# A row bias moved from TensorE into the residual buffer, with the residual added by an accumulating DMA

## The chip, the cores and the metric

The kernel runs on 8 cores of one Trainium2 chip. Core c computes half h = c mod 2 of sequence c // 2, so every core does the same work on 2048 rows of its own (and a few rows around them). The cores don't talk to each other. The metric is the device time of the slowest core, in microseconds.

## What is computed

One layer on x of shape (4, 4096, 1024), float32: windowed attention with 16 query heads and 2 key heads, a layer norm of the sum with x, a gated feed-forward block that mixes each row with the row before it, and a second layer norm.

```python
q, k, v = x @ Wq + bq, x @ Wk + bk, x @ Wv + bv        # 16, 2 and 2 heads of 64
scores = einsum('bgrsd,bgswd->bgrsw', qg, k_win)       # a window of 256 keys about each row
out = softmax(scores) @ v_win
x1 = layernorm(x + out @ Wo + bo)
x_prev = shift(x1, 1)
r = sigmoid((mu_r * x1 + (1 - mu_r) * x_prev) @ W_r.T)
k = (mu_k * x1 + (1 - mu_k) * x_prev) @ W_k.T
y = layernorm(x1 + r * (square(relu(k)) @ W_v.T))
```

The change is about `bo`, the bias of the output projection, and about how the `x +` of the third last group of lines is brought in.

## The kernel before, in words

The work of a core is written out as 172 slots (`NSLOT`). A planner (`plan_units`, `plan_rows`) fixes ahead of time which unit of work falls in which slot, and each engine's program is a loop over the same slots. Up to slot 131, each slot holds one step of attention: TensorE makes the scores of 64 rows of two pairs of heads (`qk`, L231, L237), VectorE takes the row maxima (`max_step`, L529), ScalarE the exponentials (`exp_step`, L383), VectorE scales them (`normalise`, L534, L541). Every fourth slot TensorE multiplies by the values (`av`, L344) and ScalarE evicts the result into `ao` (`ao_out`, L441). Beside these steps the slots hold units of projections: K and V (L270), q (L276), the feed-forward products k, r, v (L301, L309, L319), and the output projection o. Their results go through three PSUM banks in turn (`pm`), evicted by ScalarE or VectorE, and a unit waits for the eviction of the unit three before it.

**The output projection.** For each of 17 blocks tau of 128 rows there are two units ("o", tau, 0) and ("o", tau, 1), one for each half of the 1024 columns. They stand in slots 15, 16 for tau = 0 and 8 tau + 10, 8 tau + 11 for the others. Each is eight products `ao` x `w16o` of 128x128 by 128x512 (L289), and a ninth product of a single row, `ones` (1x128) by `bo16` (1x512), which adds the bias (L291). VectorE then adds `zx`, which holds x, and writes the sum back into `zx` with a row total (L565). `zx` has two buffers, tau mod 2.

**The first layer norm.** ScalarE squares `zx` in slot SQ1[tau] (`squares_1`, L464), GpSimd computes mean and scale with 128x1 operations (`layer_norm`, L675 to L687), ScalarE writes the normalised rows into `qy` in slot YOUT[tau] = SQ1[tau] + 2 (`rows_y`, L469). Then `zx` is free, and x of block tau + 2 is loaded into it: GpSimd waits for `s_y` in slot YOUT[tau] + 1 and issues the DMA (L698). The first two blocks are loaded after the weights w16o (L662). YOUT is 19, 22, 30, 38, 46, 54, 62, 70, 79, 86, 94, 102, 110, 118, 126 for the fifteen blocks that a load follows.

**The second layer norm.** Its squares stand in slots SQ2 (73, 76, 87, 88, 99, 103, 112, 115, 125, 128, ...; `squares_2`, L481), GpSimd computes its scale one slot later in program order (L725 to L728, the operations at L678 to L687), and ScalarE writes the rows two slots after SQ2, in slots FIN (75, 78, 89, 90, 101, 105, 114, 117, ...; `rows_out`, L486).

**The queues.** GpSimd issues, in program order: w16k, four pieces of x for group 0, the four pieces of wq with mask and ident between them, w16v, x of group 1, w16o, the bias, the first two `zx`; then, slot by slot, first the first layer norm, then the load of `zx` (L698), then at most one piece of x or of the feed-forward weights, then the second layer norm. SyncE (SP) issues `cols`, and then slot by slot: from slot 73 on, in every odd slot, a DMA transpose of probabilities (`p_transpose`, L739), due at the `av` four or so slots later; in slots 48 + 13 h and 50 + 13 h a DMA transpose of normalised rows (`y_transpose`, L747), which needs the transpose before it into the same buffer to have landed (L746), and which VectorE needs for `shift_diff` (L591, L595) in slot 52 + 13 h; and the output DMA after each FIN (L767). All DMAs of a core share its 16 DMA engines.

Of the kernel before, what the change touches and what calls it, by code (L numbers as in the profile page):

```python
# [9 lines left out]
ALU = mybir.AluOpType  # L10

D = 1024
KC = 8
# [96 lines left out]
def build_nc():  # L110
# [19 lines left out]
    wkf_in = dram("wkf", [KC, 128, D])  # L130
    wvf_in = dram("wvf", [KC, 128, D])
    cols_in = dram("cols", [128, 32])
    bo_in = dram("bo", [1, D])
    mask_in = dram("mask", [128, 2, 64])
    ident_in = dram("ident", [128, 256])
    out = dram("out", [T, D], "ExternalOutput")
# [21 lines left out]
    junk = sb("junk", [128, D])  # L158
    mask = sb("mask_s", [128, 2, 64])
    ident = sb("ident_s", [128, 256])  # L160
    bo16 = sb("bo16", [1, D])
    ones = sb("ones", [1, 128])
    cols = sb("cols_s", [128, 32], F32)
    bkm = sb("bkm", [128, 4], F32)
    nmax = sb("nmax", [128, 4, 2], F32)
# [25 lines left out]
    mur_s, muk_s = cols[:, 12:20], cols[:, 20:28]  # L191


    d_cols, d_mask, d_ident, d_bo = sem("d_cols"), sem("d_mask"), sem("d_ident"), sem("d_bo")
    d_wk, d_wv, d_wo = sem("d_wk"), sem("d_wv"), sem("d_wo")
    d_wr, d_wkf, d_wvf = sem("d_wr"), sem("d_wkf"), sem("d_wvf")
    d_wq = [sem("d_wq%d" % j) for j in range(4)]
# [23 lines left out]
    def tensor(e):  # L221
# [19 lines left out]
        def unit(u):  # L241
# [38 lines left out]
            elif kind == "o":  # L280
                if b == 0:
                    e.wait_ge(s_ao, 2 * a + 1)
                if a == 0 and b == 0:
                    e.wait_ge(s_cst, 1)
                if a == 0 and b == 0:
                    e.wait_ge(d_wo, 128)
                    e.wait_ge(d_bo, 16)
                for kc in range(KC):
                    e.matmul(pm[:, bank, :], ao[:, a % 2, kc, :], w16o[:, kc, 512 * b:512 * b + 512],  # L289
                             start=(kc == 0), stop=False)  # L290
                mm = e.matmul(pm[:, bank, :], ones[:, :], bo16[:, 512 * b:512 * b + 512],  # L291
                              start=False, stop=True)
            elif kind == "k":
                if b == 0:
                    e.wait_ge(s_mix, 8 * a + 8)
                if a == 0 and b == 0:
                    e.wait_ge(d_wkf, 128)
                for j in range(2):
                    dc = 2 * b + j
                    for kc in range(KC):  # L300
                        mm = e.matmul(pm[:, bank, 256 * j:256 * j + 256],  # L301
                                      w16kf[:, kc, 128 * dc:128 * dc + 128],
                                      xk[a % 2][:, kc, :],
                                      start=(kc == 0), stop=(kc == KC - 1))
            elif kind == "r":
                if a == 0 and b == 0:
                    e.wait_ge(d_wr, 128)
                for kc in range(KC):
                    mm = e.matmul(pm[:, bank, :],  # L309
                                  xr[(a // 2) % 2][:, kc, 128 * (a % 2):128 * (a % 2) + 128],  # L310
                                  w16r[:, kc, 512 * b:512 * b + 512],
                                  start=(kc == 0), stop=(kc == KC - 1))
            else:
                if a % 2 == 0 and b == 0:
                    e.wait_ge(s_ka, 4 * (a // 2) + 4)
                if a == 0 and b == 0:
                    e.wait_ge(d_wvf, 128)
                for kc in range(KC):
                    mm = e.matmul(pm[:, bank, :],  # L319
                                  kact[(a // 2) % 2][:, kc, 128 * (a % 2):128 * (a % 2) + 128],  # L320
                                  w16vf[:, kc, 512 * b:512 * b + 512],
                                  start=(kc == 0), stop=(kc == KC - 1))
# [190 lines left out]
                    evac(u)  # L513

    def vector(e):
        e.memset(ones[:, :], 1.0)
        e.memset(vt[:, 0:64], 0.0)
        e.memset(vt[:, 64 + XC:128 + XC], 0.0)
        e.memset(ao[:, 0, :, 0:64], 0.0)
# [105 lines left out]
    def gpsimd(e):  # L625
# [3 lines left out]
        def wq_piece(j):  # L629
            e.dma_start(wq[j], wq_in.ap()[j]).then_inc(d_wq[j], 16)  # L630

        def wo_piece(c):
            e.dma_start(w16o[:, c, :], wo_in.ap()[c]).then_inc(d_wo, 16)

# [22 lines left out]
        e.wait_ge(d_xt[1], 64)  # L657
        for c in range(5, 8):
            wo_piece(c)
        e.dma_start(bo16[:, :], bo_in.ap()).then_inc(d_bo, 16)  # L660
        for j in range(2):
            e.dma_start(zx[:, j, :], xres.ap()[128 * j:128 * j + 128, :]).then_inc(d_xres[j], 16)  # L662

        def small(ins, s=s_p):
            nonlocal n_p
# [24 lines left out]
        for n in range(NSLOT):  # L690
            if n - 1 in SQ1:
                tau = SQ1.index(n - 1)
                e.wait_ge(s_sq1, tau + 1)
                layer_norm(st1[:, tau % 2, :], True, tau == 0, s_ln1)
            if n - 1 in YOUT[:NT - 2]:
                tau = YOUT.index(n - 1)
                e.wait_ge(s_y, tau + 1)
                e.dma_start(zx[:, tau % 2, :], xres.ap()[128 * (tau + 2):128 * (tau + 3), :]) \  # L698
                    .then_inc(d_xres[tau % 2], 16)
            piece = 3 * ((n - 12) // 4) + (n - 12) % 4 if n >= 12 and (n - 12) % 4 < 3 else -1  # L700
            if 0 <= piece < 36:
                e.wait_ge(s_ex, n)
# [26 lines left out]

    def sync(e):  # L730
        e.dma_start(cols[:, :], cols_in.ap()).then_inc(d_cols, 16)

        def p_transpose(b, pair):
            r = b % 2
# [15 lines left out]
        for n in range(NSLOT):  # L750
# [4 lines left out]
            if 0 <= h < NH and f in (0, 2):  # L755
# [3 lines left out]
                if f == 0 and h >= 1:  # L759
                    e.wait_ge(s_pc, h)  # L760
                y_transpose(2 * h + 1 + f // 2, par, 64 * f, 2 * (h // 2) + par + f // 2)
            if n - 1 in FIN:
                r = FIN.index(n - 1)
                e.wait_ge(s_o, r + 1)
# [54 lines left out]
def _host_inputs(L0_attn_x, L0_attn_Wq, L0_attn_bq, L0_attn_Wk, L0_attn_bk,  # L819
# [16 lines left out]
        wr=_by_chunks(np.asarray(L0_ffn_W_r, np.float32).T),  # L836
        wkf=_by_chunks(np.asarray(L0_ffn_W_k, np.float32).T),
        wvf=_by_chunks(np.asarray(L0_ffn_W_v, np.float32).T),
        bo=np.ascontiguousarray(np.asarray(L0_attn_bo, np.float32).reshape(1, D)),
        mask=mask,  # L840
        ident=np.concatenate([np.tile(np.eye(64, dtype=np.float32), (2, 2)),
                              np.eye(128, dtype=np.float32)], 1),
# [38 lines left out]
```

## Time and profile before

| what | value |
|---|---|
| time, median of 3 runs | 510.87 us (510.54 to 511.59) |
| the profiled execution's own time | 509.77 us |
| its span on the slowest core (core 5) | 508.2 us |
| spans of the 8 cores | 504.9 to 508.2 us |
| busy: TensorE / ScalarE / VectorE / GpSimd | 87% / 66% / 62% / 21% of the span |
| granted TensorE clock, mean | 0.960 of full speed |
| DMA: moved, mean rate | 48.25 MB, 95 GB/s |

The span is first to last instruction of one core; the device time of the same execution is 1.57 us longer. Busy shares are means over stages with different limits. In a row that merges instructions, the first number is the start and the second the time to the end of the last of them.

### The profile page before, as it was taken

Reading aid. Unit: us, or ns where it says so; the run is one execution under the profiler, and the core shown is the slowest. Engines: PE = TensorE matmul, PEld = TensorE weight load, DVE = VectorE, ACT = ScalarE, POOL = GpSimd, SP = SyncE. Lnnn points to the kernel's source line nnn. Section 1 sums busy time; section 2 is a strip of 40 time slices with the busy share of each in tenths; the row PEclk is TensorE's granted clock in tenths of the full one; section 3 lists DMA queues with packets and bytes.
Section 4 is the critical chain, followed back from the end, with each engine's and each line's share of the span. In section 5 each row is a group of like instructions: output and inputs, shape, how many; then the busy total and the mean of one; then the engine's idle time right before and its main releaser. Section 6 shows DMA issues by size and latency. Waiting matters only on the chain.

```text
span 508.2 us, 10503 instructions; the slowest of 8 cores (504.9 to 508.2 us)
## 1 busy us (share of the span) xinstructions
PE 440.9 (87%) x3052; PEld 220.6 (43%) x3052; DVE 316.5 (62%) x793; ACT 333.3 (66%) x847; POOL 109.0 (21%) x298
## 2 busy tenths in 40 slices
PE   0779999999899869798898988998979988999990
PEld 0344444444444345444363353353435345464640
DVE  0056765654655587576967877877776896545421
ACT  1267868686768575776679496669658769446542
POOL 4330124130403030101122230121123032130303
PEclk9996999999999878899999999999989999999996
DMA  8999429939263646100265286567254548303112
GB/s 108 164 164 195 62 44 115 161 64 140 28 110 54 113 73 117 40 5 1 66 139 135 52 100 156 110 84 187 53 115 115 135 53 177 90 1 103 43 42 83
DMA packets 71448, 48.25 MB, mean 95 GB/s; under 512 B 59104, under 2 KB 60256, under 8 KB 71392
## 3 DMA queue, kind: packets, MB, share of 16 engines
q0 software_dynamic: 11632, 24.88, 28.1%
q1 hardware_dynamic: 59760, 22.70, 22.7%
q8 instruction: 26, 0.43, 0.4%
q14 instruction: 30, 0.25, 0.2%
HBM read 40.85 MB, written 8.39 MB: 97 GB/s over the span
## 4 chain that ended last, share of the span: by engine, by line
PE 59%; ACT 15%; DVE 9%; issue 8%; DMA 5%; POOL 1%; ACTq 0%; SPq 0%; DVEq 0%; POOLq 0%
PE pm L289 11%; PE pm L276 8%; PE pm L319 8%; PE pm L309 6%; PE pm L301 6%; PE po L344 6%; ACT p L383 5%; PE psc L231 4%; DVE nmax L529 4%; PE pm L255 3%; DMA bufq<-wq 2%; PE pm L291 2%; ACT junk L464 2%; DMA yT<-qy 2%; PE pm L270 1%
## 5 line engine op out<-in xcount | busy, mean ns | idle before, releaser
L383 ACT ACTIVATE p<-psc,nmax 128x320 bf16<-128x320 f32 x264 | 138.8, 540 | 96.1 <-DVE nmax L529 95.9
L529 DVE TENSOR_REDUCE nmax<-psc 128x2 f32<-128x640 f32 x132 | 108.1, 821 | 88.8 <-PE psc L237 88.2
L289 PE MATMUL pm<-w16o,ao 128*128 128x512 bf16 x272 | 66.3, 388 | 2.5 <-ACT ao L441 1.2
L541 DVE TENSOR_SCALAR p<-p,rall 128x320 bf16<-128x320 bf16 x264 | 62.4, 299 | 7.6 <-DVE rall L534 0.7
L276 PE MATMUL pm<-bufx,bufq 128*128 128x512 bf16 (+2 forms) x320 | 65.1, 350 | 1.7 <-DMA bufq<-wq 1.7
L301 PE MATMUL pm<-bufx,w16kf 128*128 128x256 bf16 x512 | 62.4, 278 | 2.1 <-ACT pt L397 1.5
L309 PE MATMUL pm<-w16r,bufx 128*128 128x512 bf16 x256 | 59.6, 379 | 5.0 <-DVE zx L565 2.2
L319 PE MATMUL pm<-w16vf,bufq 128*128 128x512 bf16 x256 | 59.5, 380 | 1.8 <-ACT pt L397 1.8
L383 ACT ACTIVATION_READ_ACCUMULATOR p<-psc,nmax 128x1 f32 x264 | 57.1, 216 | 0.0
L301 PEld LDWEIGHTS pm<-bufx,w16kf 128*128 128x128 bf16 x512 | 48.7, 99 | 14.1 <-issue 8.0
L231 PE MATMUL psc<-k,qy 64*128 64x320 bf16 x264 | 41.7, 313 | 13.5 <-ACT p L383 13.1
L276 PEld LDWEIGHTS pm<-bufx,bufq 128*128 128x128 bf16 x320 | 28.6, 100 | 30.0 <-issue 9.4
L255 PE MATMUL pm<-ident_s,p 128*128 128x128 bf16 x360 | 34.2, 230 | 7.2 <-ACT qy L421 4.8
L289 PEld LDWEIGHTS pm<-w16o,ao 128*128 128x128 bf16 x272 | 24.9, 98 | 33.4 <-issue 8.5
L676 POOL TENSOR_TENSOR st<-st 128x1 f32<-128x1 f32 x17 | 3.8, 224 | 162.5 <-ACT junk L464 162.5
L571 DVE SCALAR_TENSOR_TENSOR zb<-bufq,pm 128x512 f32<-128x512 f32 x32 | 21.8, 683 | 26.6 <-PE pm L319 26.6
L309 PEld LDWEIGHTS pm<-w16r,bufx 128*128 128x128 bf16 x256 | 23.2, 97 | 33.7 <-issue 9.4
L344 PE MATMUL po<-pt,v 128*64 128x256 bf16 (+1 forms) x396 | 37.0, 292 | 0.2 <-issue 0.2
L565 DVE SCALAR_TENSOR_TENSOR zx<-pm,zx 128x512 f32<-128x512 f32 x34 | 23.4, 688 | 21.5 <-PE pm L291 21.3
L319 PEld LDWEIGHTS pm<-w16vf,bufq 128*128 128x128 bf16 x256 | 23.3, 98 | 30.6 <-issue 5.5
L255 PEld LDWEIGHTS pm<-ident_s,p 128*128 128x128 bf16 x360 | 23.9, 102 | 23.4 <-issue 20.1
L231 PEld LDWEIGHTS psc<-k,qy 64*128 64x128 bf16 x264 | 13.2, 93 | 41.7 <-issue 34.4
(80 smaller groups left out, 572.4 us busy)
## 6 DMA issues: line engine op xcount, KB each, us to landing
zx<-xres POOLq DMA_DIRECT2D x17, 512.0 KB, 6.3
out<-zb SPq DMA_DIRECT2D x16, 512.0 KB, 3.2
bufx<-xt POOLq DMA_DIRECT2D x16, 256.0 KB, 8.9
bufq<-wq POOLq DMA_DIRECT2D x4, 512.0 KB, 10.0
w16o<-wo POOLq DMA_DIRECT2D x8, 256.0 KB, 11.8
w16kf<-wkf POOLq DMA_DIRECT2D x8, 256.0 KB, 5.8
w16r<-wr POOLq DMA_DIRECT2D x8, 256.0 KB, 6.1
w16vf<-wvf POOLq DMA_DIRECT2D x8, 256.0 KB, 6.5
```

The costliest lines, as they stand in the source:

```text
L231: e.matmul(psc[:, 2 * (n % 2) + g, 0:320], qb[64 * g:64 * g + 64, b + 1, 2 * j:2 * j + 2, :], k16[64 * g:64 * g + 64, 64 * b:64 * b + 320] ...
L255: mm = e.transpose(pm16[:, bank, 128 * c:128 * c + 128], src[:, 128 * c:128 * c + 128], eye)
L276: mm = e.matmul(pm[:, bank, 0:QHI[a] - QLO[a]], wq[b // 2][:, kc, 128 * (b % 2):128 * (b % 2) + 128], xt[:, a % 2, kc, QLO[a]:QHI[a]], sta ...
L289: e.matmul(pm[:, bank, :], ao[:, a % 2, kc, :], w16o[:, kc, 512 * b:512 * b + 512], start=(kc == 0), stop=False)
L301: mm = e.matmul(pm[:, bank, 256 * j:256 * j + 256], w16kf[:, kc, 128 * dc:128 * dc + 128], xk[a % 2][:, kc, :], start=(kc == 0), stop=(kc ...
L309: mm = e.matmul(pm[:, bank, :], xr[(a // 2) % 2][:, kc, 128 * (a % 2):128 * (a % 2) + 128], w16r[:, kc, 512 * b:512 * b + 512], start=(kc ...
L319: mm = e.matmul(pm[:, bank, :], kact[(a // 2) % 2][:, kc, 128 * (a % 2):128 * (a % 2) + 128], w16vf[:, kc, 512 * b:512 * b + 512], start=( ...
L344: mm = e.matmul(po[64 * g:64 * g + 64, :].rearrange("p (s k q) -> p k s q", k=2, q=128)[:, kind, :, :], v16[lo:hi, (b + kind) % 2, vc, 64 ...
L383: a = e.activation(p16[:, b % 2, j // 2, g, j % 2, :], psc[:, 2 * (n % 2) + g, 0:320], AF.Exp, bias=nmax[:, n % 4, g:g + 1], accum_out=sal ...
L529: e.tensor_reduce(nmax[:, n % 4, :], psc[:, 2 * (n % 2):2 * (n % 2) + 2, 0:320], mybir.AxisListType.X, ALU.max, negate=True).then_inc(s_mx, 1)
L541: t = e.tensor_scalar(part, part, rall[:, b % 2, r:r + 1], None, ALU.mult)
L565: e.scalar_tensor_tensor(z, src, 1.0, z, ALU.mult, ALU.add, accum_out=st1[:, a % 2, b:b + 1]).then_inc(s_ed, 1)
```

## The change

`bo` becomes an input of 128 equal rows (`np.tile` on the host), 512 KB. The products of `ones` by `bo16` are gone, with both tiles, the memset of `ones` and the load of `bo16` (2 KB) on GpSimd. SyncE copies the 128 bias rows into `zx` (a "fill"): both buffers right at the start after `cols`, and later in slot YOUT[tau] + 1 once `rows_y` of block tau is done. GpSimd waits for the fill (`d_bo`) and then issues the load of x as a DMA that adds to what is in `zx`: for the first two where they stood, for the others one slot later than before, YOUT[tau] + 2. In a slot that holds both, it comes after the first layer norm and ahead of the second one, as before. Within SyncE's slot the fill comes after `p_transpose` and `y_transpose` and ahead of the output DMA. The bias fills read 17 x 512 KB more from memory.

```diff
-    bo_in = dram("bo", [1, D])
+    bo_in = dram("bo", [128, D])
...
-    bo16 = sb("bo16", [1, D])
-    ones = sb("ones", [1, 128])
...
-                    e.wait_ge(d_bo, 16)
                 for kc in range(KC):
-                    e.matmul(pm[:, bank, :], ao[:, a % 2, kc, :], w16o[:, kc, 512 * b:512 * b + 512],
-                             start=(kc == 0), stop=False)
-                mm = e.matmul(pm[:, bank, :], ones[:, :], bo16[:, 512 * b:512 * b + 512],
-                              start=False, stop=True)
+                    mm = e.matmul(pm[:, bank, :], ao[:, a % 2, kc, :], w16o[:, kc, 512 * b:512 * b + 512],
+                                  start=(kc == 0), stop=(kc == KC - 1))
...
     def gpsimd(e):
+        def add_xres(tau):
+            e.wait_ge(d_bo[tau % 2], 16 * (tau // 2 + 1))
+            e.dma_start(zx[:, tau % 2, :], xres.ap()[128 * tau:128 * tau + 128, :],
+                        accum_op=ALU.add).then_inc(d_xres[tau % 2], 16)
...
-        e.dma_start(bo16[:, :], bo_in.ap()).then_inc(d_bo, 16)
         for j in range(2):
-            e.dma_start(zx[:, j, :], xres.ap()[128 * j:128 * j + 128, :]).then_inc(d_xres[j], 16)
+            add_xres(j)
...
-            if n - 1 in YOUT[:NT - 2]:
-                tau = YOUT.index(n - 1)
-                e.wait_ge(s_y, tau + 1)
-                e.dma_start(zx[:, tau % 2, :], xres.ap()[128 * (tau + 2):128 * (tau + 3), :]) \
-                    .then_inc(d_xres[tau % 2], 16)
+            if n - 2 in YOUT[:NT - 2]:
+                add_xres(YOUT.index(n - 2) + 2)
...
     def sync(e):
         e.dma_start(cols[:, :], cols_in.ap()).then_inc(d_cols, 16)
+        for j in range(2):
+            e.dma_start(zx[:, j, :], bo_in.ap()).then_inc(d_bo[j], 16)
...
                 y_transpose(2 * h + 1 + f // 2, par, 64 * f, 2 * (h // 2) + par + f // 2)
+            if n - 1 in YOUT[:NT - 2]:
+                tau = YOUT.index(n - 1)
+                e.wait_ge(s_y, tau + 1)
+                e.dma_start(zx[:, tau % 2, :], bo_in.ap()).then_inc(d_bo[tau % 2], 16)
```

## Rows read from the trace of the kernel before

**Rows 1.** The page: span, TensorE's busy time, the chain that ended last
```profile
span 508.2 us, 10503 instructions; the slowest of 8 cores (504.9 to 508.2 us)
PE 440.9 (87%) x3052; PEld 220.6 (43%) x3052; DVE 316.5 (62%) x793; ACT 333.3 (66%) x847; POOL 109.0 (21%) x298
...
PE 59%; ACT 15%; DVE 9%; issue 8%; DMA 5%; POOL 1%; ACTq 0%; SPq 0%; DVEq 0%; POOLq 0%
PE pm L289 11%; PE pm L276 8%; PE pm L319 8%; PE pm L309 6%; PE pm L301 6%; PE po L344 6%; ACT p L383 5%; PE psc L231 4%; DVE nmax L529 4%; PE pm L255 3%; DMA bufq<-wq 2%; PE pm L291 2%; ACT junk L464 2%; DMA yT<-qy 2%; PE pm L270 1%
```
**Rows 2.** Line L291: count, shortest/median/longest in ns, first and last start
```profile
L291 PE MATMUL pm<-bo,ones x34: 384/385/602, 63.7 to 450.8; 1*128 1x512 bf16 x34
```
**Rows 3.** Timeline of TensorE about one bias product (start, us, engine, line)
```profile
63.69 0.39 PE L291 MATMUL pm<-bo,ones 1*128 1x512 bf16 x1
64.01 0.45 PE L255 MATMUL pm<-ident_s,p 128*128 128x128 bf16 x5
```
**Rows 4.** Timeline of the start: first DMAs, TensorE's first two waits
```profile
1.06 0.39 SPq L731 DMA_DIRECT2D cols_s<-cols  x1
1.55 0.74 POOL L635 DMA_DIRECT2D w16k<-wk  x1 [0.87 <-POOLq L111]
...
14.05 3.26 PE L270 MATMUL pm<-bufx,w16k 128*128 128x512 bf16 x8 [14.05 <-DMA bufx<-xt]
...
21.59 1.46 PE L276 MATMUL pm<-bufx,bufq 128*128 128x384 bf16 x8 [1.68 <-DMA bufq<-wq]
```
**Rows 5.** Stretches: PE, PEld, DVE, ACT, POOL busy, PEclk, DMA share, GB/s
```profile
0.00:2.00 2.00, 0.00 (x0) 0.00 (x0) 0.80 (x5) 0.94 (x1) 0.63 (x5) 1.00 0.00 0
6.00:8.00 2.00, 0.00 (x0) 0.00 (x0) 0.00 (x0) 0.00 (x0) 0.63 (x2) 1.00 1.12 161
244.00:245.00 1.00, 1.00 (x8) 0.34 (x8) 1.00 (x4) 0.00 (x0) 0.00 (x0) 1.00 0.65 115
245.00:246.00 1.00, 1.00 (x15) 0.50 (x14) 0.60 (x1) 0.00 (x0) 0.00 (x0) 1.00 0.97 397
```
**Rows 6.** The page's DMA issues: KB each, median us from issue to landing
```profile
zx<-xres POOLq DMA_DIRECT2D x17, 512.0 KB, 6.3
out<-zb SPq DMA_DIRECT2D x16, 512.0 KB, 3.2
```
**Rows 7.** Timelines of ACT, SP and POOL about slots 86 to 89
```profile
293.69 1.24 ACT L469 ACTIVATE qy<-zx,st 128x1024 bf16<-128x1024 f32 x1
...
289.48 7.14 SPq L739 DMA_TRANSPOSE pt<-p  x2
296.82 1.45 SPq L747 DMA_TRANSPOSE yT<-qy  x1
...
295.48 0.62 POOL L698 DMA_DIRECT2D zx<-xres  x1 [3.16 <-ACT qy L469]
297.15 0.18 POOL L678 TENSOR_SCALAR st<-st 128x1 f32<-128x1 f32 x1 [1.05 <-ACT junk L481]
...
299.31 0.29 POOL L687 TENSOR_TENSOR st<-st 128x1 f32<-128x1 f32 x1
...
301.64 1.27 ACT L486 ACTIVATE zb<-zb,st 128x1024 f32<-128x1024 f32 x1
```
**Rows 8.** Timelines of SP, POOL and ACT about slots 103 to 105
```profile
344.34 7.39 SPq L739 DMA_TRANSPOSE pt<-p  x2
...
349.79 0.26 POOL L687 TENSOR_TENSOR st<-st 128x1 f32<-128x1 f32 x1
...
351.70 1.34 ACT L486 ACTIVATE zb<-zb,st 128x1024 f32<-128x1024 f32 x1
```
**Rows 9.** Waits for transposes: VectorE and TensorE timelines, the chain
```profile
309.18 0.18 DVE L591 COPY yT<-yT 128x8 bf16<-128x8 bf16 x1 [3.43 <-DMA yT<-qy]
...
312.46 1.89 PE L309 MATMUL pm<-w16r,bufx 128*128 128x512 bf16 x8 [1.42 <-DVE zx L565]
...
421.20 6.25 DMA yT<-qy
```

More of the change, by code:

```diff
@@ L191, in build_nc @@
     mur_s, muk_s = cols[:, 12:20], cols[:, 20:28]
-    d_cols, d_mask, d_ident, d_bo = sem("d_cols"), sem("d_mask"), sem("d_ident"), sem("d_bo")
+    d_cols, d_mask, d_ident = sem("d_cols"), sem("d_mask"), sem("d_ident")
+    d_bo = [sem("d_bo%d" % j) for j in range(2)]
     d_wk, d_wv, d_wo = sem("d_wk"), sem("d_wv"), sem("d_wo")
@@ L515, in vector @@
     def vector(e):
-        e.memset(ones[:, :], 1.0)
         e.memset(vt[:, 0:64], 0.0)
@@ L838, in _host_inputs @@
         wvf=_by_chunks(np.asarray(L0_ffn_W_v, np.float32).T),
-        bo=np.ascontiguousarray(np.asarray(L0_attn_bo, np.float32).reshape(1, D)),
+        bo=np.ascontiguousarray(np.tile(np.asarray(L0_attn_bo, np.float32).reshape(1, D), (128, 1))),
         mask=mask,
```

## The prediction

> **What bounds the kernel now.** I read the page first, then the chain of waits, then the timelines of the places that the edits touch. TensorE is busy 440.9 of 508.2 us [rows 1], and the chain that ended last lies on it for 59% of the span, on ScalarE for 15%, on VectorE for 9%, on DMA for 5% [rows 1]. So TensorE is what mostly sets the pace, with ScalarE close behind: time taken from TensorE is worth something, and time added to ScalarE costs something. The line of the bias products, L291, has 2% of that chain [rows 1], about 10.2 us. At the start nothing computes: TensorE first waits 14.05 us for weights and x, and again for wq until 21.59 [rows 4]; the DMA engines' share in the stretch from 6 to 8 us is over 1 [rows 5]. That stage is bound by DMA, and the change puts 1 MB into it.
>
> The times below are those of the profiled execution: 508.2 us span, 509.77 us device time, 1.10 us below the median of 510.87. I sum against 509.77 and carry the difference to the median.
>
> **Taken away: 34 bias products.** Each lasts 385 ns [rows 2] and overlaps the next. What the path gives is from start to start: L291 starts at 63.69, the unit after it at 64.01 [rows 3], so 0.32 us each, 34 x 0.32 = 10.9 us in all. The chain's 10.2 us say that 32 of the 34 were on it. Not all of that comes back. Once TensorE is ahead, ScalarE (333.3 us busy, and in some slots without a gap) or the loop scores, maxima, exponentials holds it at the next wait. Upper bound 10.9 us; as lower bound I take half of the chain's share, 5 us, which would need a shadow behind every second product. TensorE's 59% against ScalarE's 15% put it nearer the upper end: **-8.0**. The wait for `bo16` and the memset go too; the weight load dominates the wait and the memset precedes the first DMA landing, so 0.
>
> **Added at the start: two fills of 512 KB.** What one costs the DMA engines I read from a load of the same size in a quiet place: one at 242.67 us (the eighth of fifteen at its line) shows as shares of 0.65 and 0.97 of two successive microseconds [rows 5], so 1.6 to 1.7 us of all 16 engines. Two make 3.4 us. SyncE is free from 1.45 us [rows 4], before GpSimd's first load can get going, and until 2 us the engines do nothing [rows 5]. About 1 us of the fills may fall into this gap; the rest pushes w16k, x and wq back, and with them all that follows. Bounds 0 (the fills fit in gaps) and +3.4; nearest is the row of the full DMA stretch, so **+2.5**. That stretch writes 161 GB/s as bf16, read as twice as many bytes of f32 [rows 5], some 320 GB/s.
>
> The Trainium skill, page "HBM Reference", section "Specifications (TRN2)", gives a core about 358 GB/s when both cores of a pair stream. By that rule 1.05 MB cost an estimated 2.9 us, not 3.4, and the sum would be half a microsecond better at most; the trace's 320 GB/s lies below that limit.
>
> **Moved: SyncE's fill, then GpSimd's wait for it.** A fill goes the way of the output DMA: same queue, size and partitions, 3.2 us from issue to landing [rows 6]. Upper bound is the 6.3 us of the loads of x [rows 6]. The GpSimd load used to need `s_y` only. Now GpSimd stands still until the fill has landed, with the second layer norm queued behind it where SQ2 follows YOUT closely. The planner's numbers give two such places, slots 88 and 104; at 112/113 and 128/129 the squares come a slot later and cover most of the wait, and early on only weight pieces stand behind it, all due many slots later.
>
> *Slot 88.* `rows_y` ends at 294.93, but in slot 87 SyncE first issues two transposes; the second of them starts at 296.82 and takes 1.45 [rows 7]. So the fill is issued at about 298.4, behind them in the same queue, and lands 3.2 to 3.6 later, at about 302. GpSimd then issues the adding load (0.62 us) and starts the layer norm at 302.8. That took from 297.15 to 299.60 [rows 7], 2.45 us, so it ends at 305.3. ScalarE wants it at 301.64 [rows 7]: a stall of 3.7 us. The next layer norm (SQ2 88) then ends at 307.8 and is wanted at 304.78 + 3.7, no second stall. Against it stands a wait that may shrink: `y_transpose`, issued at 296.82 next to the load of x, landed so late that VectorE lost 3.43 us at 309.18, and TensorE 1.42 us [rows 9]. The load of x no longer collides with it, and the path has that much slack. Taken: 3.7 - 1.4, about **+2.5** (0 if the fill slips ahead and ScalarE had other slack, +6 with a landing of 6.3).
>
> *Slot 104.* `p_transpose` starts at 344.34 [rows 8], issued for 1.35 us; the fill lands at about 349.2, the load is issued, the layer norm ends at 352.3 to 352.8. It ended at 350.05 and is wanted at 351.70 [rows 8]: 1.1 us of stall, of which part is slack: **+0.6** (0 to +3.6).
>
> **More traffic beside the transposes.** Per block the engines now carry a fill (1.7 us) and an adding load. What such a load costs no row shows. Bounds: 1.7 us, that of a plain one, and 3.4, if both streams that it reads count in full. I take 2. Loads are due at slot 8 tau + 26 and are issued ten slots before; 6.3 us plus 3 are hidden there, and for the first one (five slots, some 13 us) just so. The `d_bo` of the first two was served long before. The transposes are not so covered: the one at 421.20, on the chain, took 6.25 us [rows 9] beside a load of x. Now a fill stands right ahead of it in its queue instead, and the add comes after it. Taken: **+0.8** (-1.5 if the collision goes, +4 if three or four places lose 1 us each).
>
> The Trainium skill, page "DMA: Bandwidth & Descriptors", section "SDMA does more than copy", says that the DMA engines add in units inline with the data stream; by that rule the adding load costs what a plain one does. No run here shows it yet.
>
> **SyncE's waits.** The fills put waits for `s_y` ahead of `y_transpose` 0 to 4, which ran far ahead before. The fill of slot 47 waits to about 162 us, their consumer stands in slot 52, after 179: some 10 us of room, cost 0; without that room VectorE would wait.
>
> **Sum:** -8.0 + 2.5 + 2.5 + 0.6 + 0.8 = -1.6 us. 509.77 becomes 508.2; the median 510.87 becomes **509.3 us**.
>
> **The rivals.**
>
> *The fills are hidden.* The first DMA data would flow before w16k wants the engines, GpSimd's wait would end in time, and TensorE's gain comes whole: -10.2 + 1 + 1.5 + 0.5 = -7.2, to about 503.7; half way, 505.5. For it: TensorE's share of the chain. Against it: the full DMA stretch at the start, and the order in SyncE's slot 87.
>
> *GpSimd's hold decides (slower).* Its place is the wait for the fill ahead of the layer norm in slots 88 and 104, its price the landing time. At 6.3 us, as for the loads of x, the stalls are 6.4 - 1.4 = 5.0 and 3.6 us, the sum -8.0 + 2.5 + 5.0 + 3.6 + 0.8 = +3.9, or 514.8. It turns the sign from a landing of about 4.5 us. For it: these fills are issued right behind transposes, when the engines are busy. Against it: 3.2 us for the output DMA on the same queue. With a landing of 5.5 it is about 513.
>
> *The gain is absorbed.* TensorE's 0.32 us are lost each time to ScalarE, the gain is 5 to 6 us, the losses as above: +0.5 to +1.4, so 511.3 to 512.3. For it: ScalarE runs without a gap in the stretch about slots 88 and 104. Against: 32 of 34 products on the chain.
>
> **How the numbers follow.** Forecast case, 507.5 to 511: chance 0.45. Fills hidden, 503.5 to 507: 0.20. GpSimd's hold, 512 to 515: 0.20. Gain absorbed, 510.5 to 512.5: 0.15. About 0.2%, 1 us, is what a measurement can tell from no change here. Faster by more: 0.28 of the forecast case and the 0.20, 0.48. Within: 0.15 of the forecast case and 0.08 of the absorbed one, 0.23. Slower: 0.02 + 0.20 + 0.07, 0.29. The range 505.0 to 514.0 leaves out the far end of each side, and its halves follow the bounds: 4.3 us down are the full gain with half-hidden fills, 4.7 up a landing of near 6 us.
>
> **What would show it.** L291 is gone and 34 units are 0.32 us shorter. TensorE's first product moves from 14.05 to about 16.5. In slots 88 and 104 ScalarE's L486 waits for GpSimd's L687, by about 3.7 and 1.1 us, and GpSimd waits for a DMA into `zx`. The landing of fills (3.2 to 3.6) and of adding loads (6 to 8). A start that does not move, fills that land in over 4.5 us, or no wait at L486 would make it wrong, each with a step of its own.

## The result: slower by 2%, and the profile after

The changed kernel takes 1.0195 times the time of before, 95% interval 1.0163 to 1.0226; its median is 521.03 us. It is slower beyond doubt; whether by more than 2% the interval leaves open. Ratios and intervals compare executions in which all cores held their usual clock: in two of five of the changed kernel a die or both ran at a lower one, and these took 541 and 560 us. In the profiled execution the device time is 521.47 us, 11.7 us above the 509.77 of before. The forecast was 509.3 with a range up to 514.0, so both the sign and the size were wrong.

The page after: span, engines, the chain that ended last by engine and by line, the two DMA queues, the group of the adding loads, and three lines of DMA issues.

```profile
span 519.8 us, 10424 instructions; the slowest of 8 cores (508.3 to 519.8 us)
PE 428.0 (82%) x2976; PEld 221.8 (43%) x3018; DVE 316.7 (61%) x792; ACT 332.6 (64%) x847; POOL 113.0 (22%) x297
...
q0 software_dynamic: 11600, 24.88, 30.9%
q1 hardware_dynamic: 62208, 31.61, 27.2%
...
PE 51%; DMA 11%; DVE 11%; ACT 11%; issue 9%; POOL 3%; SPq 2%; ACTq 0%; DVEq 0%; POOLq 0%
PE pm L287 9%; PE pm L275 8%; PE pm L305 7%; PE pm L315 7%; DMA yT<-qy 5%; PE po L340 5%; PE pm L297 5%; PE psc L230 4%; DVE nmax L524 4%; ACT p L379 3%; PE pm L254 3%; DMA bufq<-wq 2%; DMA zx<-bo 2%; DMA w16k<-wk 2%; ACT junk L460 2%
...
L629 POOL DMA_DIRECT2D zx<-xres x17 | 15.4, 928 | 117.7 <-DMA zx<-bo 116.7
...
zx<-bo SPq DMA_DIRECT2D x17, 512.0 KB, 4.5
zx<-xres POOLq DMA_DIRECT2D x17, 512.0 KB, 6.5
out<-zb SPq DMA_DIRECT2D x16, 512.0 KB, 3.1
```

Three things are to be seen against [rows 1]. TensorE's busy time fell (440.9 to 428.0 us; some records of this core are missing), while the span grew by 11.6. On the chain TensorE fell from 59% to 51%, and DMA rose from 5% to 11%, GpSimd from 1% to 3%: what TensorE gave, waits took. And the spans of the cores, which lay within 3.3 us of each other, now lie within 11.5. The metric is the slowest core, so this spread is part of the loss: on the mean of the eight cores the span grew by 6.8 us and not by 11.6. A fill lands in 4.5 us at the median, not in the 3.2 of the output DMA [rows 6].

To find where the time went, I read the starts of `rows_y` and `rows_out` on ScalarE's timeline, whose slots are known, and took differences. In us, mean of the eight cores of each profiled execution ("a" is the changed kernel, e1 to e12 are the experiments below); the last row is the slowest core:

| stretch | before | e1 | a | e2 | e3 | e10 | e12 | e8 | e9 | e5 |
|---|---|---|---|---|---|---|---|---|---|---|
| to slot 19 | 76.3 | 75.9 | 77.8 | 78.5 | 78.7 | 77.9 | 78.2 | 75.0 | 74.8 | 75.6 |
| 46 to 54 | 26.1 | 25.3 | 29.9 | 24.8 | 30.5 | 31.4 | 31.5 | 33.2 | 25.6 | 24.8 |
| 86 to 89 | 7.9 | 7.9 | 13.1 | 13.5 | 7.9 | 7.9 | 9.6 | 8.0 | 7.9 | 7.9 |
| 89 to 94 | 17.1 | 17.1 | 15.9 | 16.6 | 15.6 | 14.8 | 17.9 | 17.5 | 17.3 | 16.3 |
| 102 to 105 | 8.7 | 8.7 | 11.5 | 12.2 | 8.7 | 8.7 | 10.0 | 8.7 | 8.7 | 8.7 |
| 105 to 110 | 15.4 | 14.5 | 15.5 | 15.2 | 14.5 | 14.5 | 14.2 | 14.5 | 14.6 | 14.5 |
| 127 to 130 | 8.7 | 8.7 | 11.3 | 11.5 | 8.7 | 11.6 | 8.7 | 8.7 | 8.7 | 8.7 |
| 130 to 134 | 10.5 | 10.5 | 8.2 | 8.2 | 10.7 | 7.9 | 10.5 | 10.7 | 10.5 | 10.8 |
| to slot 168 | 500.1 | 490.3 | 507.0 | 504.5 | 497.9 | 497.9 | 502.8 | 497.2 | 489.4 | 489.5 |
| slowest core | 501.6 | 494.1 | 513.3 | 508.6 | 503.4 | 502.1 | 505.3 | 505.2 | 491.1 | 495.7 |

The fair comparison is with e1, the kernel before without its bias products. Against it the changed kernel loses 4.6 us about slot 52, 5.1 before slot 89, 2.9 before slot 105 and 0.9 right behind it, 2.7 before slot 130, and 1.9 at the start. Not all of it stays: from 89 to 94 it is 1.1 us shorter than e1, and from 130 to 134 it is 2.3 shorter, so that the wait before slot 130 is made up but for 0.3 us.

The cores differ in more than one stretch. Between core 2 (508.8 us) and core 6 (519.8) 2.5 us lie in 46 to 54, 3.0 in 38 to 46 and 1.7 in 105 to 110, and the last two go with TensorE's clock. After the wait before slot 105 it fell on six cores and stayed up on cores 2 and 4. The stretch 105 to 110 on core 2 and on core 6, with columns as in [rows 5]:

```profile
354.68:368.90 14.22, 12.36 (x74) 5.14 (x75) 9.69 (x26) 10.02 (x28) 2.04 (x7) 1.00 0.49 114
```
```profile
360.91:376.82 15.91, 13.89 (x73) 5.54 (x75) 9.22 (x25) 10.01 (x29) 2.04 (x7) 0.89 0.45 104
```

**Slot 88.** The timelines of SyncE, GpSimd and ScalarE of core 6, and two stretches with their columns as in [rows 5]:

```profile
299.74 1.28 SPq L745 DMA_TRANSPOSE yT<-qy  x1
301.11 0.54 SPq L763 DMA_DIRECT2D zx<-bo  x1
...
306.04 0.90 POOL L629 DMA_DIRECT2D zx<-xres  x1 [10.82 <-DMA zx<-bo]
306.70 0.47 POOL L677 TENSOR_SCALAR st<-st 128x1 f32<-128x1 f32 x1
...
309.35 0.19 POOL L686 TENSOR_TENSOR st<-st 128x1 f32<-128x1 f32 x1 [0.43 <-POOL st L685]
...
309.63 1.24 ACT L482 ACTIVATE zb<-zb,st 128x1024 f32<-128x1024 f32 x1 [4.97 <-POOL st L686]
...
308.00:310.00 2.00, 0.00 (x0) 0.00 (x0) 0.00 (x0) 0.37 (x1) 1.26 (x5) 0.78 0.55 83
310.00:312.00 2.00, 0.50 (x2) 0.26 (x3) 0.00 (x0) 2.00 (x5) 1.15 (x5) 0.50 1.05 209
```

This is the chain that the prediction worked out for [rows 7]: transposes, then the fill at 301.11, GpSimd's issue only at 306.04, the layer norm, and ScalarE 4.97 us late. From the fill's issue to GpSimd's next step it is 4.9 us and not 3.6. TensorE then has nothing to do from 305.7 to 311.5, and when it goes on its granted clock is 0.50, the lower of its two levels (1.2 and 2.4 GHz), for some 4 us.

**Slot 52.** The timelines of SyncE and VectorE and the chain (start, us, what) of the same core:

```profile
78.77 84.40 SPq L763 DMA_DIRECT2D zx<-bo  x5
163.27 11.69 SPq L745 DMA_TRANSPOSE yT<-qy  x3
...
165.41 7.29 DMA yT<-qy
172.77 12.22 DMA yT<-qy
...
185.22 0.24 DVE L586 COPY yT<-yT 128x8 bf16<-128x8 bf16 x1 [6.74 <-DMA yT<-qy]
```

The three transposes of rows 0 to 2, which had left at 77, 87 and 111 us, now leave from 163.27, right behind the fifth fill. They have some 15 us; but one lands after 7.29 us, the next, which must wait for it, after 12.22, and VectorE stands still for 6.74 us; on the eight cores it is 4.1 to 7.7.

That such a transpose can take this long stood already in the trace before. There, on core 5, the same three leave beside weights and x and take 11.0 to 15.8 us, which nobody notices, as they are wanted only at 179 us. The line of DMA issues for the stretch 76 to 113 us of core 5 before (median to landing):

```profile
yT<-qy SPq DMA_TRANSPOSE x3, 11.4
```

### The profile page after: what moved, and what is told of

The parts are those of the page before. It is cut to its first block, busy times and chain, and to the rows that moved or that the text cites. A ratio compares the mean times of both kernels' runs of the same rounds, so it can differ in the third digit from the quotient of the medians.

```text
span 519.8 us, 10424 instructions; the slowest of 8 cores (508.3 to 519.8 us)
## 1 busy us (share of the span) xinstructions
PE 428.0 (82%) x2976; PEld 221.8 (43%) x3018; DVE 316.7 (61%) x792; ACT 332.6 (64%) x847; POOL 113.0 (22%) x297
## 4 chain that ended last, share of the span: by engine, by line
PE 51%; DMA 11%; DVE 11%; ACT 11%; issue 9%; POOL 3%; SPq 2%; ACTq 0%; DVEq 0%; POOLq 0%
PE pm L287 9%; PE pm L275 8%; PE pm L305 7%; PE pm L315 7%; DMA yT<-qy 5%; PE po L340 5%; PE pm L297 5%; PE psc L230 4%; DVE nmax L524 4%; ACT p L379 3%; PE pm L254 3%; DMA bufq<-wq 2%; DMA zx<-bo 2%; DMA w16k<-wk 2%; ACT junk L460 2%
## 5 line engine op out<-in xcount | busy, mean ns | idle before, releaser
L315 PE MATMUL pm<-w16vf,bufq 128*128 128x512 bf16 x247 | 58.1, 379 | 2.9 <-ACT pt L393 2.0
L379 ACT ACTIVATION_READ_ACCUMULATOR p<-psc,nmax 128x1 f32 x264 | 55.5, 210 | 0.0
L230 PE MATMUL psc<-k,qy 64*128 64x320 bf16 x264 | 41.7, 313 | 14.2 <-ACT p L379 13.9
L254 PE MATMUL pm<-ident_s,p 128*128 128x128 bf16 x360 | 33.5, 227 | 13.2 <-ACT qy L417 10.9
L287 PEld LDWEIGHTS pm<-w16o,ao 128*128 128x128 bf16 x272 | 25.3, 100 | 44.0 <-issue 20.0
L275 PEld LDWEIGHTS pm<-bufx,bufq 128*128 128x128 bf16 x320 | 29.3, 102 | 31.3 <-issue 11.6
L629 POOL DMA_DIRECT2D zx<-xres x17 | 15.4, 928 | 117.7 <-DMA zx<-bo 116.7
L305 PEld LDWEIGHTS pm<-w16r,bufx 128*128 128x128 bf16 x256 | 23.9, 99 | 35.1 <-issue 11.3
L340 PE MATMUL po<-pt,v 128*64 128x256 bf16 (+1 forms) x396 | 38.4, 300 | 0.1
L254 PEld LDWEIGHTS pm<-ident_s,p 128*128 128x128 bf16 x360 | 24.8, 101 | 29.8 <-issue 23.2
L560 DVE SCALAR_TENSOR_TENSOR zx<-pm,zx 128x512 f32<-128x512 f32 x34 | 23.4, 687 | 15.8 <-PE pm L287 15.4
```

Of the source, the lines that this page charges most:

```text
L230: e.matmul(psc[:, 2 * (n % 2) + g, 0:320], qb[64 * g:64 * g + 64, b + 1, 2 * j:2 * j + 2, :], k16[64 * g:64 * g + 64, 64 * b:64 * b + 320] ...
L254: mm = e.transpose(pm16[:, bank, 128 * c:128 * c + 128], src[:, 128 * c:128 * c + 128], eye)
L275: mm = e.matmul(pm[:, bank, 0:QHI[a] - QLO[a]], wq[b // 2][:, kc, 128 * (b % 2):128 * (b % 2) + 128], xt[:, a % 2, kc, QLO[a]:QHI[a]], sta ...
L287: mm = e.matmul(pm[:, bank, :], ao[:, a % 2, kc, :], w16o[:, kc, 512 * b:512 * b + 512], start=(kc == 0), stop=(kc == KC - 1))
L305: mm = e.matmul(pm[:, bank, :], xr[(a // 2) % 2][:, kc, 128 * (a % 2):128 * (a % 2) + 128], w16r[:, kc, 512 * b:512 * b + 512], start=(kc ...
L315: mm = e.matmul(pm[:, bank, :], kact[(a // 2) % 2][:, kc, 128 * (a % 2):128 * (a % 2) + 128], w16vf[:, kc, 512 * b:512 * b + 512], start=( ...
```

## The experiments

### The first term alone, and three repairs, one at a time

**e1_no_bias.** The kernel before, without the bias products:

```diff
-                    e.matmul(pm[:, bank, :], ao[:, a % 2, kc, :], ...
-                mm = e.matmul(pm[:, bank, :], ones[:, :], bo16[:, ...], start=False, stop=True)
+                    mm = e.matmul(pm[:, bank, :], ao[:, a % 2, kc, :], ..., stop=(kc == KC - 1))
```

> The kernel before with the 34 bias products left out and nothing else changed; the output lacks bo. It measures the first term of the sum by itself. If the term was right (-8.0 of at most 10.9 us), the ratio to before is 0.984, about 502.7 us. If TensorE's time is mostly absorbed by ScalarE, it is 0.990 or more (-5 us or less), and then part of the loss of the changed kernel is a gain that never came.

Measured: 0.9804 (0.9782 to 0.9826), 10.0 us less. Nearly all of TensorE's 10.2 us on the chain came back; the mean span of the cores over the fast executions fell by 10.9 us, the full 34 x 0.32. So what the change adds costs 1.0195 - 0.9804, 0.039 or 20 us.

**e2_early_y.** The first three transposes of rows leave ahead of the fills:

```diff
-            if 0 <= h < NH and f in (0, 2):
+            if n - 1 in YOUT[:3]:
+                y_transpose(*[(0, 1, 128, 0), (1, 0, 0, 0), (2, 0, 64 * 2, 1)][YOUT.index(n - 1)])
+            if 1 <= h < NH and f in (0, 2):
...
-                if h == 0 and f == 0:
-                    y_transpose(0, 1, 128, 0)
```

> The changed kernel with y_transpose 0, 1 and 2 put into SyncE's program right ahead of the first three fills, so that they no longer stand behind the fill of slot 47. Holds theory (SyncE's waits for s_y keep these transposes back until 163 us, and VectorE waits for them in slot 52): VectorE's wait at L586 in slot 52 goes, the time from rows_y of slot 46 to that of slot 54 falls from 28.7 to 31.2 us on the cores looked at back to 26, and the ratio to before falls from 1.0195 by 0.005 to 0.009. Traffic theory (more bytes on the DMA engines make every transfer late, wherever it is issued): no more than 0.002.

Measured: 1.0082 (1.0052 to 1.0112), 0.0113 or 5.8 us less than the changed kernel. The stretch 46 to 54 takes 24.8 us on the mean of the cores, and VectorE waits for a transpose in slot 52 on none of them. Its timeline on core 4:

```profile
179.12 0.17 DVE L586 COPY yT<-yT 128x8 bf16<-128x8 bf16 x1
```

**e3_late_add.** The adding loads behind the second layer norm, two slots later:

```diff
-            if n - 2 in YOUT[:NT - 2]:
+            if n - 2 in YOUT[:7]:
                 add_xres(YOUT.index(n - 2) + 2)
...
                 layer_norm(st2[:, r % 2, :], False, False, s_ln2)
+            if n - 4 in YOUT[7:NT - 2]:
+                add_xres(YOUT.index(n - 4) + 2)
```

> The changed kernel with the adding loads from the eighth on moved behind the second layer norm and two slots later in GpSimd's program, so that no layer norm of slots 88, 104 and 129 waits for a fill; bytes and fills are the same. Holds theory: rows_out in slots 89, 105 and 130 no longer waits for GpSimd, which is 5.0, 2.8 and 2.6 us from the milestones: ratio 1.0195 - 0.018 = 1.001 (1.001 to 1.007 if the waits were half in each other's shadow). Traffic theory: the stretches 86 to 89, 102 to 105 and 127 to 130 stay long, 1.015 or more.

Measured: 0.9998 (0.9976 to 1.002), 0.0197 or 10.1 us less, with every byte still moved. This edit changes the order and also the slot of the loads; e10 below changes the order alone. The stretches before 89, 105 and 130 are back at 7.95, 8.65 and 8.67. The same place as above, on core 3, timelines of GpSimd, ScalarE and SyncE:

```profile
304.13 0.19 POOL L686 TENSOR_TENSOR st<-st 128x1 f32<-128x1 f32 x1
...
307.72 0.90 POOL L629 DMA_DIRECT2D zx<-xres  x1 [0.34 <-issue]
...
306.57 1.26 ACT L482 ACTIVATE zb<-zb,st 128x1024 f32<-128x1024 f32 x1
...
303.16 0.51 SPq L765 DMA_DIRECT2D zx<-bo  x1
```

The layer norm is done at 304.32, 2.2 us before ScalarE wants it, though the fill was issued just 1 us before that. The load itself is issued late and nobody misses it.

**e4_late_start.** The first two fills wait for x of group 1:

```diff
+        e.wait_ge(d_xt[1], 64)
         for j in range(2):
             e.dma_start(zx[:, j, :], bo_in.ap()).then_inc(d_bo[j], 16)
```

> The changed kernel with the first two fills held on SyncE until x of group 1 has landed, so that nothing is added to the DMA load of the start. If the fills delay the start and the delay stays to the end, TensorE's first product moves from 17.3 back to 14 us and the ratio falls by 0.006 (3 us), to 1.0135. If the delay is made up later (it was 1.5 us by slot 19 in the trace after), the ratio falls by 0.003 or less.

Measured: 1.0175 (1.014 to 1.0209), 0.002 or 1 us less, which the intervals can't tell from nothing. On the mean of the cores of the profiled executions it is 2.2 us at slot 19 and 2.0 at slot 168, so the delay of the start was not made up there. TensorE's first product stood at 17.29 in the changed kernel on core 6 (14.05 before [rows 4]); here, on core 5:

```profile
15.10 3.57 PE L269 MATMUL pm<-bufx,w16k 128*128 128x512 bf16 x8 [15.10 <-DMA bufx<-xt]
```

### Do the repairs add up, and what is left

**e5_all_three.** The edits of e2, e3 and e4 together.

> The three repairs of e2_early_y, e3_late_add and e4_late_start together, on the changed kernel. If they act at different places and add up: 1.0195 - 0.0113 - 0.0197 - 0.0020 = 0.9865, about 504 us, faster than both kernels. What then stands above the 0.9804 of e1_no_bias, 0.006 or 3 us, is what the fills and adding loads cost by their traffic alone. If one wait only hides another (the transposes being late anyway), the sum does not come: 0.993 or more.

Measured: 0.9817 (0.9787 to 0.9847), median 501.62 us. This version beats both kernels. It lies 0.0013 above e1_no_bias, well inside the intervals, which leave room for about 2 us either way: the traffic of seventeen fills and adding loads costs nothing here that can be measured, net of what their new places save.

One core of the profiled execution, core 3, lost 8.6 us of VectorE's time in slot 91. A transpose of rows issued at 293.51 landed after 12.0 us, with an adding load issued 0.6 us behind it:

```profile
305.63 0.19 DVE L586 COPY yT<-yT 128x8 bf16<-128x8 bf16 x1 [8.61 <-DMA yT<-qy]
```

That core sets the time of this execution, 503.87 us, the longest of the six.

**e6_two_orders.** The edits of e2 and e3, with the fills at the start.

> The changed kernel with the early transposes and the late adding loads, but with the two fills at the start as the change has them. Against e5_all_three it shows the price of the fills at the start where nothing else is late. If the 3 us by which TensorE starts later stay to the end, the ratio is 0.006 above that of e5_all_three; if they are mostly made up, as e4_late_start says, 0.002.

Measured: 0.9861 (0.9837 to 0.9884), 0.0044 or 2.2 us above e5_all_three. The intervals touch; the two ways to measure the start term, this and e4, give 2.2 and 1.0 us. On the mean of the cores they give 2.0 and 3.1 us. So the start costs some 2 to 3 us, as forecast; how much of it the slowest core shows was not settled.

**e7_add_no_fill.** The kernel of e1 with loads that add; x is added to what was left in `zx`:

```diff
-                e.dma_start(zx[:, tau % 2, :], xres.ap()[...]) \
+                e.dma_start(zx[:, tau % 2, :], xres.ap()[...], accum_op=ALU.add) \
```

> The kernel of e1_no_bias with the fifteen later loads of zx made adding ones, at their old place; no fills, no new waits. The values are wrong, since x is added to what was left in zx. It isolates the adding load: 0.90 against 0.62 us of GpSimd's time for each issue, and its reading of zx. If adding costs the DMA engines little more than copying: 0.9804 to 0.983. If it takes twice the engines' time and meets the transposes: 0.986 or more.

Measured: 0.9843 (0.9817 to 0.987), 0.0039 or 2.0 us above e1, between the two expectations and with overlapping intervals. On the mean of the cores the stretch 130 to 134 is 1.5 us longer (12.1 against 10.5), and there a transpose of rows leaves about 1 us behind an adding load; the time to slot 168 is 0.9 us longer. The queue's line on the page, first of this kernel (span 501.4 us), then of e1_no_bias (500.7 us):

```profile
q0 software_dynamic: 11632, 24.88, 31.7%
```
```profile
q0 software_dynamic: 11632, 24.88, 29.0%
```

158.9 against 145.2 us of the 16 engines: 13.7 us for 15 loads, 0.9 us more for each in this traffic. The median landing rose from 6.0 to 7.1 us.

### Why slot 52 cost so much

**e8_sync_waits.** The kernel of e1, with SyncE's waits but no fills:

```diff
+            if n - 1 in YOUT[:NT - 2]:
+                e.wait_ge(s_y, YOUT.index(n - 1) + 1)
```

> The kernel of e1_no_bias with SyncE's fifteen waits for s_y put in where the change has its fills, and no fill issued; loads of x as before. It isolates the order on SyncE from the traffic. Holds theory: the transposes 0 to 2 leave at 160 us as in the changed kernel, VectorE waits in slot 52, and the ratio is 0.9804 + 0.0113 = 0.992 (0.988 to 0.993). Traffic theory: 0.982 or less.

Measured: 1.003 (1.0008 to 1.0051). Fifteen waits on an engine that computes nothing, with not a byte moved more, cost 0.0226 or 11.5 us against e1. Expected were 5.8; both theories were too low, and the holds theory is the one whose mechanism is seen. The loss lies in the stretch 46 to 54: 33.2 us on the mean of the cores against 25.3 in e1, and 39.65 on core 3, the slowest, whose chain and stretch read:

```profile
161.23 22.15 DMA yT<-qy
183.45 6.99 DMA yT<-qy
...
188.00:190.00 2.00, 0.00 (x0) 0.00 (x0) 0.00 (x0) 0.00 (x0) 0.00 (x0) 0.50 1.36 175
```

A transpose issued at 161.23 landed after 22.15 us, and the one after it could only then be issued. From 188 to 190 us no engine computes, while the DMA engines' share is 1.36. Why this costs more than in the changed kernel was not tried; the rows show that here the load of x leaves at 160.26, together with the transposes, and there on core 6 only at 171.44, after its fill.

**e9_quiet_transposes.** The kernel of e8, with nine weight pieces later:

```diff
+            late = {56: (27, 33), 57: (28, 34), 58: (29, 35), 59: (30,), 60: (31,), 61: (32,)}.get(n, ())
+            if piece >= 27:
+                piece = -1
...
-            if 28 <= piece < 36:
-                e.dma_start(w16vf[:, piece - 28, :], wvf_in.ap()[piece - 28]).then_inc(d_wvf, 16)
+            for p in late:
...
+                    e.dma_start(w16vf[:, p - 28, :], wvf_in.ap()[p - 28]).then_inc(d_wvf, 16)
```

> The kernel of e8_sync_waits with the last piece of w16r and the eight of w16vf issued in slots 56 to 61 and not 48 to 58, so that transposes 0 to 2, which still leave at 160 us, have only the load of x beside them. If it is the traffic of the weights that makes the late transposes land late (7 to 22 us each in the traces): VectorE's wait in slot 52 falls from 10 us or more to under 2, and the ratio from 1.003 to 0.983 to 0.988. If it is their late start alone: within 0.004 of 1.003.

Measured: 0.9808 (0.9786 to 0.9829), 0.0222 less: all of it is gone. On core 0 the transposes leave from 160.39 on, as late as in e8, and VectorE finds them there:

```profile
176.23 0.18 DVE L589 COPY yT<-yT 128x8 bf16<-128x8 bf16 x1
```

So it does on six cores; on cores 4 and 6 it still waits, 2.67 and 2.11 us. The first two transposes take 8 to 15 us even here, beside the load of x and the weights issued just before them; it is the third that now lands in 3 to 4. So it takes two things: the transposes leave late, and further loads of weights are in flight where they then leave. Either alone costs nothing that the ratios can tell: e9 lies 0.0004 above e1, and in e1 the same transposes take 7.5 to 16.4 us beside weights and x, but long before they are wanted. The Trainium skill, page "DMA: Bandwidth & Descriptors", section "Issuing engines are not separate DMA queues", says that DMAs of all issuing engines run on the same 16 engines and interleave; by that rule GpSimd's weights can hold up SyncE's transposes, and e8 against e9 agrees, with 11.3 us.

### What the hold of GpSimd consists of

**e10_norm_first.** In its own slot, the adding load behind the second layer norm:

```diff
-            if n - 2 in YOUT[:NT - 2]:
-                add_xres(YOUT.index(n - 2) + 2)
...
                 layer_norm(st2[:, r % 2, :], False, False, s_ln2)
+            if n - 2 in YOUT[:NT - 2]:
+                add_xres(YOUT.index(n - 2) + 2)
```

> The changed kernel with one edit: the adding load stands behind the second layer norm of its slot, still in slot YOUT + 2 and still waiting for its fill. Holds theory, by places: slot 104 is relieved (2.8 us), slot 129 is not (its layer norm is a slot later), and in slot 88 the first of two layer norms is relieved and the second then waits (2 to 4 of 5 us come back). Ratio 1.0195 less 0.009 to 0.013, that is 1.006 to 1.010. If the whole of e3_late_add came from giving the fills more time and not from the order, it stays at 1.016 or more.

Measured: 0.9998 (0.9978 to 1.0017), as good as e3, and better than expected. Place by place the expectation held: 102 to 105 is 8.66 on core 0, 127 to 130 stays long at 11.33, and in slot 90 the second layer norm is late. What it missed is that these two waits are mostly made up. On the mean of the cores the stretch 90 to 94 takes 9.9 us where e3 takes 12.5, and 130 to 134 takes 7.9 against 10.7. GpSimd and ScalarE about slot 90, core 0:

```profile
308.91 0.90 POOL L629 DMA_DIRECT2D zx<-xres  x1 [3.52 <-DMA zx<-bo]
...
311.93 0.29 POOL L686 TENSOR_TENSOR st<-st 128x1 f32<-128x1 f32 x1
...
312.31 1.24 ACT L482 ACTIVATE zb<-zb,st 128x1024 f32<-128x1024 f32 x1 [1.39 <-POOL st L686]
```

**e12_fill_first.** The fill at the head of SyncE's slot, GpSimd as in the change:

```diff
         for n in range(NSLOT):
+            if n - 1 in YOUT[:NT - 2]:
+                tau = YOUT.index(n - 1)
+                e.wait_ge(s_y, tau + 1)
+                e.dma_start(zx[:, tau % 2, :], bo_in.ap()).then_inc(d_bo[tau % 2], 16)
             b, j = divmod(n - 1, 4)
             if BT <= b < NB and j in (0, 2):
                 p_transpose(b, j // 2)
...
-            if n - 1 in YOUT[:NT - 2]:
-                tau = YOUT.index(n - 1)
-                e.wait_ge(s_y, tau + 1)
-                e.dma_start(zx[:, tau % 2, :], bo_in.ap()).then_inc(d_bo[tau % 2], 16)
```

> The changed kernel with the fill moved to the head of its slot in SyncE's program, ahead of p_transpose and y_transpose; GpSimd's program as in the change. If the length of GpSimd's wait comes from the two transposes that SyncE issues first (the fill of slot 87 left 4.5 us after rows_y began, and the layer norm was wanted 5 us before it came): in slots 89, 105 and 130 the waits shrink to 0.5, 0 and under 1 us, and the ratio is 1.0195 less 0.014 to 0.018, 1.002 to 1.006. If the fill's own landing beside the traffic is what counts, 1.012 or more.

Measured: 1.0042 (1.0017 to 1.0067), 0.0153 or 7.8 us less than the changed kernel. SyncE, GpSimd and ScalarE about slot 88, core 6:

```profile
297.45 0.34 SPq L752 DMA_DIRECT2D zx<-bo  x1
...
302.06 0.90 POOL L629 DMA_DIRECT2D zx<-xres  x1 [7.28 <-DMA zx<-bo]
...
305.65 1.24 ACT L482 ACTIVATE zb<-zb,st 128x1024 f32<-128x1024 f32 x1 [1.44 <-POOL st L686]
```

The fill leaves 1.3 us after `rows_y` began at 296.14, and not 4.5, and ScalarE waits 1.44 us in place of 4.97. Its landing still takes 4.6 us. So some 3 of the 5 us were the transposes ahead of the fill, and the rest its own landing. The ratio came as expected, the places less so: against e1 the stretches before 89, 105 and 130 are longer by 1.6, 1.3 and 0 us on the mean of the cores, where 0.5, 0 and under 1 were expected.

### A cheaper combination that is less sure

**e11_three_simple.** The edits of e10, e2 and e4 together.

> The candidate of small edits: e10_norm_first, e2_early_y and e4_late_start together on the changed kernel, the adding loads still in slot YOUT + 2. If the effects add up as they did in e5_all_three: 0.9817 to 0.9865, faster than both kernels. The wait of slot 129, which this one keeps and e5_all_three did not have, could cost up to 2.6 us more (0.987); if it is made up by slot 134, as the trace of e10_norm_first suggests, nothing.

Measured: 0.9895 (0.9851 to 0.9939), faster than before but by 0.008 worse than e5_all_three, and with cores from 492.8 to 507.3 us. The loss stands between slots 22 and 30. Three cores pass there as in e5 (23.4 to 23.5 us), and five, cores 0, 2, 3, 4 and 7, take 6.2 to 9.3 us more. Core 7 takes 31.37. Its chain and TensorE's timeline there:

```profile
79.55 6.59 DMA zx<-bo
86.68 16.57 DMA zx<-xres
...
104.26 3.57 PE L287 MATMUL pm<-w16o,ao 128*128 128x512 bf16 x8 [6.29 <-DVE zx L560]
```

The first adding load after a fill has five slots, from 21 to 26. Here the fill took 6.59 us and the adding load behind it 16.57, beside a transpose, weights and x, and it came too late. On the five late cores it took 14 to 17 us, on the others 7.6 to 8.2.

Up to slot 30 the program differs from that of e5_all_three in one thing: the adding load goes behind the slot's weight piece, and there it goes ahead. That order alone does not decide. e10_norm_first has it too, and all its cores passed in time, the load landing in 7.6 to 9.7 us; so did all cores of e2, e5 and e6, which have the early transposes and the other order (5.3 to 10.4 us). Only here, where both edits stand together with the late start, is the load this late. Which of them it takes was not tried.

## Why the prediction was wrong, point by point

- **Bias products, -8.0.** Measured -10.0 (e1). The mechanism was right, and the discount for ScalarE's shadow was not needed: the chain's own 10.2 us were the better number (the page's 2% is rounded, so that "32 of the 34" is closer than it can tell).
- **SyncE's waits, "some 10 us of room, cost 0".** This is the step that failed as a mechanism. The order was seen, the time of 162 us too, and the consumer after 179. What failed is the landing: two transposes in sequence were given 10 us of room and no price, while they took 7 and 12 us beside the weight pieces of slots 48 to 58. The trace before had the price, 11.0 to 15.8 us for these very transposes, and the prediction did not read it. It costs 5.8 us in the changed kernel (e2) and 11.5 us with nothing else added (e8).
- **Slot 88, +2.5.** The mechanism was right in place and direction, and one term of it was too small. The stall was worked out as 3.7 us; on the mean of the cores it is 5.1. Of the 1.4 us set against it most were there: the transpose of rows of slot 87, which had taken 9.2 us beside the load of x on core 5, lands in 3.1 on core 6, VectorE's wait of 3.43 us is gone there, and 89 to 94 is 1.1 us shorter than in e1 on the mean of the cores. Net it cost 4.0 us.
- **Slot 104, +0.6.** Worked out as a stall of 1.1 us, of which part is slack. The stall was 2.9 us, there was no slack, and the lower clock behind it took 0.9 more: 3.8 us.
- **Slot 129, 0.** ScalarE stood still for some 2.7 us there, but all but 0.3 was made up by slot 134. Zero was nearly right, though not because the later squares cover the wait.
- **What these three share** is the fill's landing: 4.5 us at the median, where I had taken 3.2 to 3.6 from an output DMA, which is mostly issued in quiet places and goes the other way, out of the core. In quiet places a fill did land in 3.5 to 3.8 us (core 6); the one of slot 88 took 4.4. With the upper bound of 6.3 it lay inside the bounds. Together the places were priced at 3.1 us, and moving the loads (e3) gave back 10.1 in the metric. The rival "GpSimd's hold decides" named this, with 4.5 us as the point from which it turns the sign; it came nearest, but had nothing for slot 52.
- **The start, +2.5.** Right. TensorE's first product moved from 14.0 to 16.9 us on the mean of the cores. At the end of the kernel 1.0 (e4) to 2.2 us (e6 against e5) are left of it in the metric, 2.0 to 3.1 on the mean of the cores.
- **Traffic, +0.8.** Measured 0.0013, or 0.7 us, within the intervals (e5 against e1); adding loads at their old place, without fills, 2.0 us (e7). But the 0.7 is with the orders mended; where an order is wrong, traffic sets its price, as e8 and e9 show.

With the measured terms the sum is -10.0 + 1.0 + 10.1 + 5.8 + 0.7 = +7.6 us, against +10.0 measured (0.0195 of 510.71). The 2.4 us left over are not explained one by one: repairs were measured with the other waits present, and these partly overlap. Part of the answer is the spread of the cores, for which the prediction had no term. From e1 to the changed kernel the mean time to slot 168 grows by 16.7 us, of which the start, slot 52, slot 88, slot 104 and slot 129 are 1.9 + 4.6 + 4.0 + 3.8 + 0.3 = 14.6; the slowest core grows by 19.2, 2.5 more than the mean.

## What to carry to other kernels

Price a moved DMA by its landing in the company that it will have at its new place, and a wait by everything that stands behind it on its queue. Here seventeen fills and adding loads were almost free, and the order in which two in-order queues waited for them cost 16 us. Look in the trace before for the same DMA in busy company: there the transposes of rows had a median of 3.2 us, and single ones took 15.8. Where a small operation can go ahead of a wait for a DMA in the same slot, put it ahead: that one edit (e10) was worth 10 us.

## What the runs showed of the hardware

- **A DMA transpose beside other DMAs can take seven times as long.** The median of a transpose of rows is 3.2 us before (core 5) and 4.0 after (core 6); the longest took 15.8 us before, and 22.15 in one core of e8, with cast loads of weights and the load of x in flight.
- **An adding load costs more than a plain one of its size,** on GpSimd 903 against 625 ns for each issue, on the DMA engines 0.9 us more than the 1.6 to 1.7 us of [rows 5]. The Trainium skill, page "DMA: Bandwidth & Descriptors", section "SDMA does more than copy", has the adding units inline with the data stream and states no cost. The prediction drew from it that adding costs the engines nothing more, and e7 against e1 does not bear that out.
- **A wait costs more than its length.** After TensorE had stood still from 305.7 to 311.5 us in slot 88, the next eight 128x512 products took 3.57 us at a granted clock of 0.50, against 1.89 at full clock [rows 9]. Behind the wait before slot 105 the same work took 15.91 us on the cores where the clock fell and 14.22 where it did not, 1.7 us for this alone. Slot 88 on core 6:

```profile
306.00:308.00 2.00, 0.00 (x0) 0.00 (x0) 0.61 (x1) 0.00 (x0) 1.52 (x4) 1.00 1.26 109
312.00:314.00 2.00, 2.00 (x6) 0.64 (x5) 1.32 (x7) 2.00 (x5) 0.00 (x0) 0.50 0.77 287
```
